# One wide edge product per sub-block in place of four column-tiled ones, in a graph-attention layer on one core

## The reference, cut to what matters

```
h = jnp.einsum('nd,hdf->nhf', x, W)
e = jax.nn.leaky_relu(a_src[src] + a_dst[dst], NEG_SLOPE)
ex = jnp.exp(e - emax[dst])
denom = jax.ops.segment_sum(ex, dst, num_segments=N)
alpha = ex / denom[dst]
msg = h[src] * alpha[:, :, None]
out = jax.ops.segment_sum(msg, dst, num_segments=N)
```

## Time and profile before

| | us |
|---|---|
| median of 3 runs (lowest, highest) | 2542.84 (2538.41, 2550.55) |
| span of the profiled execution | 2898.3 |
| PE, DVE, ACT, POOL busy in that execution | 1655.7, 1538.2, 687.3, 1778.3 |

### The profile page before, as it was taken

The page is one execution under the profiler, slowest core; times in us unless marked ns, Lnnn a source line. Parts: engine busy times, 40 slices in busy tenths (PEclk is TensorE's granted clock), DMA queues, the critical chain, the costliest instruction groups (busy, mean ns, idle before and its releaser), DMA issues. The chain is left out here.

```text
span 2898.3 us, 56530 instructions
## 1 busy us (share of the span) xinstructions
PE 1655.7 (57%) x17359; PEld 1267.0 (44%) x17359; DVE 1538.2 (53%) x5813; ACT 687.3 (24%) x2082; POOL 1778.3 (61%) x1803
## 2 busy tenths in 40 slices
PE   6566664556566334443443366765666666557894
PEld 5334433434444223332332344554554454346783
DVE  5544445556666444544544555565564655453443
ACT  4222221112221112122122123224322233323220
POOL 1666666666666666666666665656566666645774
PEclk9666565655555555555555566777777667668997
DMA  9356555534454453365365467667656765547987
GB/s 297 109 163 166 163 159 152 174 96 124 122 155 116 118 127 104 96 181 149 107 175 152 135 179 220 177 187 210 195 161 198 219 205 147 158 125 218 250 235 207
DMA packets 317811, 480.53 MB, mean 166 GB/s; under 512 B 77671, under 2 KB 241593, under 8 KB 312893
## 3 DMA queue, kind: packets, MB, share of 16 engines
q0 software_dynamic: 90960, 237.28, 31.2%
q1 hardware_dynamic: 217420, 231.05, 25.9%
q10 hardware_dynamic: 9120, 8.49, 0.9%
HBM read 399.71 MB, written 110.47 MB: 176 GB/s over the span
## 5 line engine op out<-in xcount | busy, mean ns | idle before, releaser
L1264 POOL DMA_INDIRECT region<-node_table,src_idx x1612 | 1573.9, 976 | 926.4 <-remote 489.0
L1454 PE MATMUL ps_p<-region 128*32 128x65 f32 x12896 | 405.9, 293 | 779.6 <-DVE region L1702 614.0
L1454 PEld LDWEIGHTS ps_p<-region 128*32 128x32 f32 x12896 | 311.6, 153 | 884.6 <-DVE region L1702 690.5
L1710 DVE SCALAR_TENSOR_TENSOR acc<-ps_p,region,acc 128x65 f32 x806 | 192.9, 280 | 805.1 <-remote 750.4
L1330 ACT ACTIVATE ps_p<-region 128x16 f32<-128x16 f32 x403 | 75.5, 187 | 1033.7 <-DVE region L1696 553.3
L1326 ACT ACTIVATE region<-ps_s 128x128 f32<-128x128 f32 x403 | 111.3, 276 | 835.3 <-PE ps_s L1436 384.5
L1436 PE MATMUL ps_s<-ident,region 128*128 128x128 f32 x403 | 170.2, 422 | 215.2 <-DVE region L1696 120.7
L1702 DVE TENSOR_TENSOR region<-region,ps_p 128x512 f32<-128x512 f32 x403 | 273.3, 678 | 24.0 <-ACT ps_p L1330 11.9
L1440 PEld LDWEIGHTS ps_s<-region 128*128 128x128 f32 x806 | 215.5, 294 | 75.4 <-issue 49.9
L1436 PEld LDWEIGHTS ps_s<-ident,region 128*128 128x128 f32 x403 | 105.6, 262 | 238.2 <-DVE region L1696 132.8
L1440 PE MATMUL ps_s<-region 128*128 128x32 f32 x806 | 191.0, 327 | 6.7 <-issue 6.6
(11 more groups left out here) (371 smaller groups left out, 2663.0 us busy)
## 6 DMA issues: line engine op xcount, KB each, us to landing
region<-in_W_dram SPq DMA_DIRECT2D x84, 512.0 KB
expert_in<-run_rows SPq DMA_DIRECT2D x280, 130.0 KB
region<-node_table,src_idx POOLq DMA_INDIRECT x1612
acc<-in_W_dram SPq DMA_DIRECT2D x28, 512.0 KB
region<-expert_in SPq DMA_DIRECT2D x47, 260.0 KB
acc<-base_rows SPq DMA_DIRECT2D x13, 896.0 KB
qkv_rows<-region SPq DMA_DIRECT2D x49, 194.0 KB
y_rows<-acc SPq DMA_DIRECT2D x28, 256.0 KB
```

Of the source, the lines that this page charges most:

```text
L1264: pool.indirect_dma_start(out=rows[:, s, j, :], out_offset=None, in_=table[:, :], in_offset=bass.IndirectOffsetOnAxis(ap=src_idx[:, n * SU ...
L1454: m = pe.matmul(ps_p[s % 2][h * WIN:(h + 1) * WIN, 0:HC], wts[:, s % 2, j, h, :], rows[:, s, j, h * HC:(h + 1) * HC], start=j == 0, stop=j ...
L1710: m = dve.scalar_tensor_tensor(out=a, in0=ps_p[s % 2][:, 0:HC], scalar=here[:, k, at(n)], in1=a, op0=ALU.mult, op1=ALU.add)
```

## The change

Each sub-block gets one matmul in place of four: the weights of all four heads side by side (128x128) against all 260 columns of the rows. Of the 128x260 result only the four pieces on the diagonal are wanted (head h: partitions 32h to 32h+31, columns 65h to 65h+64). They no longer lie in the same 65 columns, so ACT copies each piece into a buffer in SBUF (`head_sums`, 128 x 2 x 65), four copies a block, and DVE's `accumulate` reads this buffer. ACT does the copies of block n-1 in `body(n)`, between the exponential of block n and the mask copy of block n+2. PE waits for the copies of block n-2 (`heads_ready`) instead of DVE's `block_done`; POOL goes on waiting for `block_ps`. The exponentials move to columns 260 to 275 of the same bank. DVE's order within a block stays.

```diff
+    SUMS_W = G_HEADS * HC
...
+        head_sums = sb("head_sums", [P, 2, HC])
...
-            return ps_p[s % 2][:, P:P + SUB * G_HEADS].rearrange("p (j h) -> p j h", h=G_HEADS)
+            return ps_p[s % 2][:, SUMS_W:SUMS_W + SUB * G_HEADS].rearrange("p (j h) -> p j h", h=G_HEADS)
...
+            def own_heads(n, s):
+
+                act.wait_ge(block_ps, n + 1)
+                if n >= 2:
+                    act.wait_ge(block_done, n - 1)
+                for h in range(G_HEADS):
+                    r = slice(h * WIN, (h + 1) * WIN)
+                    m = act.activation(head_sums[r, s % 2, :], ps_p[s % 2][r, h * HC:(h + 1) * HC], ACT.Copy)
+                m.then_inc(heads_ready, 1)
+
             def body(n, s, ahead=2):
                 act.wait_ge(logits_ready, n + 1)
                 act.activation(ex_ps(s), lg[:, s % 2], ACT.Exp).then_inc(ex_ready, 1)
+                if n >= 1:
+                    own_heads(n - 1, s + SL - 1)
                 if ahead == 2 or n + 2 < BLOCKS:
                     mask_copy(n + 2, s + 2)
...
+            own_heads(BLOCKS - 1, (BLOCKS - 1) % SL)
...
                 pe.wait_ge(w_ready, n + 1)
-                if not isinstance(n, int) or n >= 2:
-                    pe.wait_ge(block_done, n - 1)
+                if n >= 2:
+                    pe.wait_ge(heads_ready, n - 1)
                 for j in range(SUB):
-                    for h in range(G_HEADS):
-                        m = pe.matmul(ps_p[s % 2][h * WIN:(h + 1) * WIN, 0:HC], wts[:, s % 2, j, h, :],
-                                      rows[:, s, j, h * HC:(h + 1) * HC], start=j == 0, stop=j == SUB - 1)
+                    m = pe.matmul(ps_p[s % 2][:, 0:SUMS_W], wts[:, s % 2, j].rearrange("p h w -> p (h w)"),
+                                  rows[:, s, j, 0:SUMS_W], start=j == 0, stop=j == SUB - 1)
                 m.then_inc(block_ps, 1)
...
-                dve.wait_ge(block_ps, n + 1)
+                dve.wait_ge(heads_ready, n + 1)
                 dve.wait_ge(block_done, n)
...
-                    m = dve.scalar_tensor_tensor(out=a, in0=ps_p[s % 2][:, 0:HC], scalar=here[:, k, at(n)], in1=a,
+                    m = dve.scalar_tensor_tensor(out=a, in0=head_sums[:, s % 2, :], scalar=here[:, k, at(n)], in1=a,
```

More of the change, by code:

```diff
@@ L1023, in main_stage @@
         self_done = sem("self_done")
+        heads_ready = sem("heads_ready")
         h_ps, h_ready, w_mean = sem("h_ps"), sem("h_ready"), sem("w_mean")
```

## The result

| | before | after |
|---|---|---|
| median, us (lowest, highest; 4 runs each) | 2543.85 (2538.41, 2550.55) | 2784.46 (2775.67, 2794.07) |
| span of the profiled execution | 2898.3 (2537.5 in a new trace, below) | 2786.2 |
| ratio, 95% interval | | 1.0946 (1.0914 to 1.0978) |

The changed kernel is 9.5% slower, 241 us. That is the forecast direction and about twice the forecast size.

The account below looks back on a forecast made before the run. It took POOL's gathers to bound light blocks and DVE's own chain full ones. Adding 94 us for full and 19 us for light blocks, 113 us, to 2542.8 gave 2656, taken as 2650 us, range 2590 to 2720.

Parts of the forecast that it names:

- The bound in the timed runs: In the block loop, bursts complete early; POOL's gathers bound light blocks, DVE's own chain full ones; 5.33 us a block.
- Burst and copies, one by one: PE's burst goes from 1.09 us to 3.82 cold or 1.92 warm; ACT's four copies take 0.7 us.
- DVE's chain: Between `logits(n)` and `accumulate(n-1)`, 1.10 us pass instead of 0.67; 218 full blocks get 0.43 us longer, 94 us.
- The light blocks: On PE's path, four in ten of 185 blocks are cold and 0.5 us too long; row buffers absorb half, leaving 19 us.
- The clock: PE's granted clock in the middle stretch rises from 0.50 to about 0.7, with cold and warm light blocks alternating.
- Rival C: All PE bursts cold: every block takes at least 5.8 us, 224 us more in all, 2765 us; chance 0.08.
- Rival B: Slower only by DVE's wait, PE's clock staying at 2.4 GHz: about 45 us more, 2590 us; chance 0.17.
- D: No change: POOL's pace hides all and light blocks even out DVE's full ones, 2543 us; chance 0.10.
- The new wait on ACT: ACT's wait for the burst of block n-1 costs nothing: PE's mask has over 2 us of cover, ACT room for 282.

Follow-up runs that it names:

- the copies alone: The changed kernel with the 16 column-tiled products put back and ACT's four copies kept: 2645.95 us beside 2546.55 for the kernel before, ratio 1.0397.
- the burst alone: The changed kernel without ACT's copies, DVE reading columns 0 to 64 from PSUM: 2577.24 us beside 2549.3 for the kernel before, ratio 1.0111.
- the turned `weigh`: The changed kernel with `weigh(n)` moved ahead of `accumulate(n-1)` in DVE's order: 2640.65 us beside 2550.7 for the kernel before, ratio 1.0355.

## Why the prediction was right and wrong

**The bound in the timed runs: right, its reason wrong.** No late completion in them, POOL at its pace of 0.30 us between gathers for most of the loop ("issue" ends the wait ahead of 1548 of 1612 gathers, 472 us), 5.31 us a block where the prediction derived 5.33. But it was not the profiler that had made the trace of before long. The check that the prediction named, a new span within 100 us of its median and below 2898, came true (2786.2 and 2784.46) and proves nothing of what it was meant for: another execution under the same profiler gives 2537.5 for the kernel before.

**Burst and copies, one by one: nearly right.** Timeline of the changed kernel, a block on PE's path:

```profile
2010.12 3.47 PE L1469 MATMUL ps_p<-region 128*128 128x260 f32 x8 [1.95 <-DVE region L1717]
...
2013.63 0.91 ACT L1338 ACTIVATE head_sums<-ps_p 32x65 f32<-32x65 f32 x4 [0.24 <-PE ps_p L1469]
2013.87 0.95 POOL L1267 DMA_INDIRECT region<-node_table,src_idx  x1 [5.44 <-PE ps_p L1469]
...
2014.68 0.48 DVE L1725 SCALAR_TENSOR_TENSOR acc<-head_sums,region,acc 128x65 f32 x2 [1.51 <-ACT head_sums L1338]
2015.08 0.68 DVE L1717 TENSOR_TENSOR region<-region,ps_p 128x512 f32<-128x512 f32 x1
...
2015.88 1.95 PE L1469 MATMUL ps_p<-region 128*128 128x260 f32 x8
```

The burst takes 3.47 us here (3.71 in the median of the 123 that took 3.3 or more) and 1.95 at full speed (forecast 3.82 and 1.92). ACT starts 0.04 us behind its end (forecast under 0.1). The copies take 0.91, not 0.7. One takes 0.215 us, as forecast (0.22); what failed is the overlap: each further one was to add 0.12 to 0.15 us, and in the trace they start 0.228 us apart in the median, one behind the other's end. From burst to burst are 5.76 us, 2.29 more than the burst, where 2.0 were forecast.

**DVE's chain: the number right, in part by luck.** The term was 94 us, and the copies alone measured 99. The chain's 1.10 us measured 1.19. But the sum had 218 full blocks at 0.43 us. From the starts of `weigh` in the traces of the copies alone and of before, the 41 blocks whose exponential first reloads ACT's table lost 0.91 us each, 37 us, and the other 361 lost 0.19 us each, 67 us. So DVE's chain proper was worth 67 of the 94, and the rest came from a kind of block that the prediction doesn't have: it found room for the copies in ACT's mean over the loop (581 of 2503 us busy), but in these 41 blocks ACT is the engine that comes last. It looks like this before:

```profile
2006.76 1.28 ACT L1330 ACT_TABLE_LOAD   x1
...
2008.06 0.19 ACT L1330 ACTIVATE ps_p<-region 128x16 f32<-128x16 f32 x1
...
2008.28 0.69 DVE L1702 TENSOR_TENSOR region<-region,ps_p 128x512 f32<-128x512 f32 x1 [2.02 <-ACT ps_p L1330]
```

and like this after:

```profile
2019.53 1.28 ACT L1343 ACT_TABLE_LOAD   x1
...
2020.83 0.19 ACT L1343 ACTIVATE ps_p<-region 128x16 f32<-128x16 f32 x1
2020.95 0.89 ACT L1338 ACTIVATE head_sums<-ps_p 32x65 f32<-32x65 f32 x4
...
2021.98 0.48 DVE L1725 SCALAR_TENSOR_TENSOR acc<-head_sums,region,acc 128x65 f32 x2 [3.52 <-ACT head_sums L1338]
...
2022.38 0.68 DVE L1717 TENSOR_TENSOR region<-region,ps_p 128x512 f32<-128x512 f32 x1
```

Before, the accumulation was done while ACT was late, and `weigh` followed the exponential by 0.22 us; after, copies and accumulation both come behind it, and it is 1.55 us.

**The light blocks: this is the step that failed.** The prediction gave PE's path (burst, copies, accumulation, `weigh`, burst) 19 us. With the copies ahead of the exponential, 144 us stay, and some 112 of them lie outside the 41 blocks of above; 125 us are lost in the 107 of these whose burst is at the low clock, and those with a burst at the high clock give 28 back. Three choices made the term small, and the traces speak to each.
- *How many.* It let four in ten of 185 blocks be cold, 74. By the records of L1469, 123 of 402 bursts took 3.3 us or more, and 225 under 2.1 us.
- *How much each.* It set a cold block at 5.8 us and its loss at 0.5, what the path is above the mean step of 5.33. The path was right: the 87 blocks that it bounds took 5.93 us. The mean was the wrong thing to compare with. The 123 cold blocks took 6.22 us where the same blocks took 5.00 in the kernel before: 1.22 us more each, 150 us together. In the 87 it is 5.93 against 4.49. The bursts are cold where a block is light, and a light block had been much shorter than the mean. The 225 warm ones (burst under 2.1 us) took 5.76 us against 5.54, 49 us together, and the 54 in between lost 39. With the same burst but no copies, the 99 cold ones took 5.45 against 5.01, and the 266 warm ones lost nothing (5.36 against 5.39).
- *Absorbed.* A mean of cold and fast below POOL's 5.03 was taken as mostly covered by the row buffers. For the burst alone that holds: 28 us measured, half of DVE's added wait. With the copies in the path it doesn't: ACT's wait for the burst is 142.4 us in 120 blocks (3.2 us with the tiled burst), and POOL's grows from 77 to 356 us.

Shown by experiment are three things: the two parts together cost 105 to 113 us more than one by one; shortening the copies gives back 178; ACT's order accounts for 96. That the rest is the serial path and, in the 41 blocks, ACT's own work is read from the traces block by block, and the turned `weigh` agrees; no run has taken PE's other work away from the path, or ACT's from the 41 blocks.

**The clock: right.** 0.50 became 0.74 in 900 to 1300 (forecast about 0.7), and fast and cold bursts alternate. Rival C had 2765 us, nearest to the result, for a reason that didn't hold: not all blocks are cold, 225 bursts ran at full speed. Rival B had all of them fast, and 123 are not. D fell with the copies alone: POOL's pace doesn't hide 0.65 us more ahead of the accumulation. The rule of the Trainium skill that was weighed (TensorEngine Tiling (Array Packing), "When to Use Tiling") agrees with the burst's own time, 1.10 against 1.95 or 3.47 us; here that alone is worth 28 us.

**The new wait on ACT: not free.** It was costed by what is queued behind it. It should have been costed by what is queued ahead too: the exponential with its wait for `logits(n)`. DVE's chain in the prediction has that for the full blocks; the edit that puts the copies ahead gives back 96 us over blocks of all kinds.

No version run here beats the kernel before.

## What to carry to other kernels

Don't add two changes' prices where they lie on one loop: a longer burst hidden by slack (28 us) and a copy in the other engine's chain (99 us) ate the same slack and cost 241. When a mean of short and long blocks stays below the bound, ask which blocks are the long ones and what those same blocks took before; the wait is paid block by block. An engine with room in the mean can still be the last one in some blocks. And a new operation on an in-order engine takes on every wait of what stands ahead of it, so weigh its place by what its input waits for.

## What the runs showed of the hardware that was not expected

- A copy of 32x65 out of PSUM takes 215 ns on ACT (L1338), one of 128x65 213 ns (L1336): cutting a copy by partitions saves nothing. Four of them take 0.89 us against 0.22, since they don't overlap (starts 0.228 us apart), where the two copies of the earlier trace rows overlap by 0.10 us.
- The wider burst lifts PE's own clock: in 900 to 1300 us from 0.50, the level of 1.2 GHz throughout, to 0.74, a mix of both levels. Over the whole loop 225 of 402 bursts take under 2.1 us and 123 take 3.3 or more.
- The same kernel has two times, 2540 to 2554 and 2905 to 2945 us, by session. In the trace of the long kind, POOL goes on 4.99 us after the start of a burst of modelled 1.09 us, and what a change costs in one says little of the other: the turned `weigh` is 3.6% slower than before in one and 2.8% in the other, the copies alone 4.0% and 1.1%.
